# Turning the short row blocks of experts 2 to 7 in pairs, and issuing gathers ahead of the older scatter

## What is computed

```python
x = x + gnn(layernorm(x), adj, W, a1, a2)          # attention over 1354 x 1354, float32
n = layernorm(x)                                    # 1354 x 512
probs = softmax(n @ Wr + br)                        # 8 experts
gate, idx = max(probs), argmax(probs)
pos = rank of the token among those of its expert   # tokens with pos >= 169 are dropped
expert_in[e, pos] = gate * n[token]                 # for the tokens of expert e
h  = relu(expert_in @ W1[e] + b1[e])                # 512 -> 512
eo = h @ W2[e] + b2[e]                              # 512 -> 512
out = x + gate * eo[idx, pos]                       # back to the token's row
```

## Time and profile before

| | us |
|---|---|
| median of 3 timed executions | 265.56 (265.4 to 267.12) |
| the profiled execution, its device time | 263.48 |
| its span in the profile | 261.7 |
| PE busy | 250.5 |
| DVE busy | 180.9 |
| ACT busy | 128.6 |
| POOL busy | 90.1 |

### The profile page before, as it was taken

How to read it: one execution, slowest core, us unless ns; L and a number is a source line. 1 busy time by engine, 2 the same in 40 slices (tenths; PEclk the granted TensorE clock), 3 DMA queues, 4 the chain that set the end, 5 groups by cost and what they waited for, 6 DMA issues and landing times.

```text
span 261.7 us, 4579 instructions
## 1 busy us (share of the span) xinstructions
PE 250.5 (96%) x1649; PEld 210.8 (81%) x1649; DVE 180.9 (69%) x429; ACT 128.6 (49%) x263; POOL 90.1 (34%) x113
## 2 busy tenths in 40 slices
PE   6799989999999999999999999999999999999990
PEld 1489989988888778778778889899977968879780
DVE  3988768996978977785762573847296685856931
ACT  2737786853765475555553121342447155454330
POOL 4334891000341432112120224118253834841502
PEclk9999999999999999999999999999999999999999
DMA  6990000320488888421211213136978679888001
GB/s 189 375 318 32 1 5 0 106 81 27 159 210 284 273 262 248 168 79 40 80 42 41 82 39 96 52 117 176 353 237 294 247 258 290 283 293 285 12 7 44
DMA packets 19210, 40.47 MB, mean 155 GB/s; under 512 B 2810, under 2 KB 3130, under 8 KB 19188
## 3 DMA queue, kind: packets, MB, share of 16 engines
q1 hardware_dynamic: 16196, 34.17, 39.5%
q0 software_dynamic: 2176, 4.80, 6.1%
q10 hardware_dynamic: 816, 1.21, 1.5%
HBM read 32.93 MB, written 8.31 MB: 158 GB/s over the span
## 4 chain that ended last, share of the span: by engine, by line
PE 87%; POOL 3%; DVE 2%; DMA 2%; issue 2%; ACT 2%; POOLq 1%; ACTq 0%
PE bank L1426 30%; PE bank L1690 12%; PE bank L1728 7%; PE bank L1364 6%; PE bank L1412 5%; PE bank L1756 5%; PE bank L1441 3%; PE bank L1660 2%; PE bank L1346 2%; DMA w_raw<-in_L_gnn_W_dram 2%; PE bank L1676 2%; PE bank L1703 2%; PE bank L1453 2%; PE bank L1464 2%; PE bank L1560 1%
## 5 line engine op out<-in xcount | busy, mean ns | idle before, releaser
L1426 PE MATMUL bank<-h_hi,pt_lo 128*128 128x512 f32 (+1 forms) x110 | 45.9, 417 | 0.0
L1426 PE MATMUL bank<-h_lo,pt_hi 128*128 128x512 f32 (+1 forms) x110 | 43.6, 396 | 0.0
L1426 PE MATMUL bank<-h_hi,pt_hi 128*128 128x512 f32 (+1 forms) x110 | 43.4, 394 | 0.0
L411 POOL TENSOR_TENSOR x_all<-x_all,w_raw 128x512 f32<-128x512 f32 x10 | 18.1, 1810 | 65.2 <-ACT w_raw L589 65.2
L1690 PE MATMUL bank<-prob,w 128*128 128x168 f32 x224 | 33.2, 306 | 0.0
L1690 PEld LDWEIGHTS bank<-prob,w 128*128 128x128 f32 x224 | 32.6, 189 | 0.7 <-issue 0.2
L754 ACT ACTIVATE adj_s<-bank,b_cols 128x168 f32<-128x168 f32 x28 | 11.3, 402 | 33.6 <-PE bank L1690 33.6
L1426 PEld LDWEIGHTS bank<-h_hi,pt_hi 128*128 128x128 f32 (+1 forms) x110 | 20.7, 188 | 4.9
L1426 PEld LDWEIGHTS bank<-h_hi,pt_lo 128*128 128x128 f32 (+1 forms) x110 | 20.7, 188 | 3.8
L1426 PEld LDWEIGHTS bank<-h_lo,pt_hi 128*128 128x128 f32 (+1 forms) x110 | 20.8, 189 | 3.6
L611 ACT ACTIVATE wide<-adj_s,off_b 128x1354 f32<-128x1354 f32 (+1 forms) x11 | 15.8, 1432 | 14.1 <-DVE off_b L887 14.1
(11 more groups left out here) (203 smaller groups left out, 558.1 us busy)
## 6 DMA issues: line engine op xcount, KB each, us to landing
w<-in_L_ffn_W_dram SPq DMA_DIRECT2D x16, 1024.0 KB, 6.7
adj_s<-in_adj_dram SPq DMA_DIRECT2D x10, 677.0 KB, 5.3
x_rows<-x_all SPq DMA_DIRECT2D x10, 257.0 KB, 3.2
out_dram<-x_all SPq DMA_DIRECT2D x10, 256.0 KB
x_all<-in_x_dram SPq DMA_DIRECT2D x9, 256.0 KB, 5.6
prob<-in_L_ffn_b_dram SPq DMA_DIRECT2D x5, 256.0 KB, 7.2
w_raw<-in_L_gnn_W_dram ACTq DMA_DIRECT2D x4, 256.0 KB, 5.5
adj_s<-in_L_ffn_b_dram SPq DMA_DIRECT2D x2, 256.0 KB, 7.0
```

The lines of the kernel that those rows point to most:

```text
L411: pool.tensor_tensor(x_all[0:R, t, 0:D], x_all[0:R, t, 0:D], relu_s[0:R, :], ALU.add).then_inc(s_x1, 1)
L1426: ins = pe.matmul(o_ps[par][0:R, :], p[0:K, par, k, 0:R], h[0:K, k, :], start=(k == 0 and n == 0), stop=(k == NT - 1 and n == 2))
```

## The change

The short blocks of experts 2 and 3, 4 and 5, 6 and 7 are put one under the other, in rows 0 to 39 and 64 to 103 of one tile, and turned as one block of PAIR = 104 rows, in the in_turn of the even expert. Expert 1 has its short block turned alone, in a block of the same 104 rows of which only the first 40 are used. The odd experts 3, 5 and 7 have only their wide block turned. To that end:
- PE: in_turn(e) has four transposes of 128 rows to bank 0, and for e = 1, 2, 4, 6 four of 104 rows to bank 1.
- DVE: prepare(e) scales the wide block by itself as soon as it has landed, and for e = 1, 2, 4, 6 then the short block or both short blocks of the pair. Scales are made one column at a time. The new counter is `s_xgt`; `s_xg` is left to expert 0.
- ACT: gx_copy(e) is one instruction of 128x512 for the wide block and, for e = 1, 2, 4, 6, one of 128x(4x40) for each short block. Its wait on `s_hid` is 2e where it was 2e - 2.
- POOL: gathers are issued by block. The short block of expert 3 is gathered with those of expert 2, and so on (two new semaphores, `s_x1n`). In the loop the wait for `s_gt` and the gathers stand ahead of scatter_out(e - 4).
- SP: the wait ahead of the weight loads is for the wide block of expert 1 alone (16 where it was 32).

```diff
@@ buffers and banks
-        xg = w_raw[:, :, 0:D].rearrange("p (i j) n -> p i j n", i=2)
+        xg_w, xg_n = (w_raw[:, 0, 0:D], w_raw[:, 2, 0:D]), (w_raw[:, 1, 0:D], w_raw[:, 3, 0:D])
+        PAIR = P // 2 + CAP - P
-        gx_ps, hid_ps, eo_ps, y_ps = ((banks[0], banks[1]), (banks[2], banks[3]),
-                                      (banks[4], banks[5]), (banks[6], banks[7]))
+        gxw_ps, gxn_ps = banks[0], banks[1]
+        hid_ps, eo_ps, y_ps = (banks[2], banks[3]), (banks[4], banks[5]), (banks[6], banks[7])
+        s_x1n = [sem("s_x1n0"), sem("s_x1n1")]
+        s_xgt = sem("s_xgt")
+        def late(e):
+            return () if e > 1 and e % 2 else (e,) if e == 1 else (e, e + 1)
+        def prepared(e):
+            return e + (e | 1) if e else 0
@@ SP
-            sp.wait_ge(s_x1g[1], 32)
+            sp.wait_ge(s_x1g[1], 16)
@@ POOL
-            def gather_x1(e):
-                for j in range(2):
-                    pool.indirect_dma_start(x1_g[e][0:S[j], j, :], None, x1_d,
-                                            bass.IndirectOffsetOnAxis(ap=src[0:S[j], j, e:e + 1], axis=0)
-                                            ).then_inc(s_x1g[e], 16)
+            def gather_x1(e, j):
+                pool.indirect_dma_start(x1_g[e][0:S[j], j, :], None, x1_d,
+                                        bass.IndirectOffsetOnAxis(ap=src[0:S[j], j, e:e + 1], axis=0)
+                                        ).then_inc(s_x1n[e // 2 % 2] if j and e else s_x1g[e], 16)
-            gather_x1(1)
-            gather_x1(2)
-            pool.wait_ge(s_x1g[1], 32)
+            gather_x1(1, 0)
+            gather_x1(1, 1)
+            gather_x1(2, 0)
+            gather_x1(2, 1)
+            gather_x1(3, 1)
+            pool.wait_ge(s_x1g[1], 16)
+            pool.wait_ge(s_x1n[0], 16)
             pool.wait_ge(s_xg, 2)
-            gather_x1(0)
+            gather_x1(0, 0)
+            gather_x1(0, 1)
             for e in range(3, E + 2):
+                if e < E:
+                    pool.wait_ge(s_gt, e - 1)
+                    gather_x1(e, 0)
+                    for i in late(e):
+                        gather_x1(i, 1)
                 if e >= 4:
                     scatter_out(e - 4)
-                if e < E:
-                    pool.wait_ge(s_gt, e - 1)
-                    gather_x1(e)
@@ ACT
             def gx_copy(e):
+                act.wait_ge(s_gt, e + 1)
+                act.wait_ge(s_hid, 2 * e)
+                ins = act.activation(gx_t[e % 2][:, :, 0:P], gxw_ps[:, :].rearrange("p (c n) -> p c n", c=KC), ACT.Copy)
+                for i, n in enumerate(late(e)):
+                    v = gxn_ps[:, 0:KC * PAIR].rearrange("p (c n) -> p c n", c=KC)
+                    ins = act.activation(gx_t[n % 2][:, :, P:CAP], v[:, :, P // 2 * i:P // 2 * i + S[1]], ACT.Copy)
                 ins.then_inc(s_gxt, 1)
@@ DVE, prepare(e)
-                dve.wait_ge(s_x1g[e], 32)
+                dve.wait_ge(s_gt, max(e - 1, 1))
+                dve.wait_ge(s_x1g[e], 16)
+                dve.tensor_tensor(scale_s[:, par, 0:1], x1_g[e][:, 0, D + 1:D + 2], gate_s[:, 0, e:e + 1], ALU.mult
                                   ).then_inc(s_scale, 1)
+                dve.wait_ge(s_scale, 2 + prepared(e - 1))
+                dve.tensor_scalar(xg_w[par], x1_g[e][:, 0, 0:D], x1_g[e][:, 0, D:D + 1], scale_s[:, par, 0:1],
+                                  ALU.subtract, ALU.mult).then_inc(s_xgt, 1)
+                if late(e):
+                    dve.wait_ge(s_x1n[e // 2 % 2], 16 * (e // 2 + 1))
+                    for n in late(e):
+                        dve.tensor_tensor(scale_s[0:S[1], n % 2, 1:2], x1_g[n][0:S[1], 1, D + 1:D + 2],
+                                          gate_s[0:S[1], 1, n:n + 1], ALU.mult).then_inc(s_scale, 1)
+                    dve.wait_ge(s_scale, 1 + prepared(e))
+                    for i, n in enumerate(late(e)):
+                        dve.tensor_scalar(xg_n[e // 2 % 2][P // 2 * i:P // 2 * i + S[1], :], x1_g[n][0:S[1], 1, 0:D],
+                                          x1_g[n][0:S[1], 1, D:D + 1], scale_s[0:S[1], n % 2, 1:2],
+                                          ALU.subtract, ALU.mult).then_inc(s_xgt, 1)
@@ PE, in_turn(e)
-                pe.wait_ge(s_xg, e * 2 + 2)
+                pe.wait_ge(s_xgt, prepared(e))
                 pe.wait_ge(s_gxt, e)
-                for j in range(2):
+                for c in range(KC):
+                    ins = pe.transpose(gxw_ps[:, c * P:(c + 1) * P], xg_w[e % 2][:, c * P:(c + 1) * P], ident[:, :])
+                if late(e):
                     for c in range(KC):
-                        o = (c % 2) * CAP
-                        ins = pe.transpose(gx_ps[c // 2][:, o + j * P:o + j * P + S[j]],
-                                           xg[0:S[j], e % 2, j, c * P:(c + 1) * P], ident[0:S[j], 0:S[j]])
+                        ins = pe.transpose(gxn_ps[:, c * PAIR:(c + 1) * PAIR],
+                                           xg_n[e // 2 % 2][0:PAIR, c * P:(c + 1) * P], ident[0:PAIR, 0:PAIR])
                 ins.then_inc(s_gt, 1)
```

More of the change, by code:

```diff
@@ L698, in _, with gx_copy_first @@
             exp_below(2)
-            def gx_copy(e):
[L701 to L704, removed]
-                for j in range(2):
[L706 to L712, removed]
+            def gx_copy_first():
+                for j in range(2):
+                    act.wait_ge((s_gt0, s_gt)[j], 1)
+                    act.activation(gx_t[0][:, 2 * j:2 * j + 2, :],
+                                   gx0_ps[j][:, 0:2 * CAP].rearrange("p (c n) -> p c n", c=2), ACT.Copy
+                                   ).then_inc((s_gx0, s_gxt)[j], 1)
+            def gx_copy(e):
+                act.wait_ge(s_gt, e + 1)
[4 more added lines that the diff above has]
+                    ins = act.activation(gx_t[n % 2][:, :, P:CAP], v[:, :, P // 2 * i:P // 2 * i + S[1]], ACT.Copy)
                 ins.then_inc(s_gxt, 1)
@@ L756, in hid_relu @@
                     ins.then_inc(s_hidv, 1)
-            gx_copy(0)
+            gx_copy_first()
             act.wait_ge(s_bc, 1)
@@ L1201, in out_bias @@
                     v = x1_g[e][0:S[j], j, 0:D]
-                    dve.wait_ge(s_xg, e * 2 + j + 1)
+                    dve.wait_ge(s_xgt, prepared(e))
                     dve.scalar_tensor_tensor(v, b2_b[i][0:S[j], :], gate_s[0:S[j], j, e:e + 1], v, ALU.mult, ALU.add
```

## The result

| | before | after |
|---|---|---|
| median of 20 timed executions | 265.63 us | 262.99 us |
| profiled execution, device time | 263.48 us | 262.5 us |
| its span | 261.7 us | 260.8 us |

The account below looks back on a forecast made before the run. PE was taken to bound the kernel; 1.65 us from the odd turns plus 0.68 from the other four gave 2.33 us off, nothing elsewhere: 265.56 - 2.33 = 263.2 us, ratio 0.991, range 262.3 to 265.2.

Parts of the forecast that it names:

- PE's bound and the odd turns: PE sets the pace; leaving the short block out of turns 3, 5 and 7 saves 0.55 us each, 1.65 us.
- The even turns: PE, turns 2, 4 and 6: a 104-row block for one of 40 takes 1.06 us for 1.23, saving 0.17 each.
- Expert 1: PE, turn of expert 1, followed by out_turn_first: the same saving of 0.17 us assumed for its 104-row block.
- The landing at expert 2: prepare(2) needs a third block: short gather lands at 186.2 to 186.9 us, stall 0; bound 1.4 us.
- C: prepare(2) late in part, landing between 187.0 and 189.2: at 188.3 a stall of 1.4 us, 264.6 us; chance 0.18.
- D: Landing for in_turn(2) so late, past 189.25, that the kernel is slower than before; chance 0.04.
- SP's earlier start: SP's weight loads of expert 2 wait for one block and start about 0.85 us earlier; 0 us for PE.
- The moved gathers: POOL issues gathers ahead of the scatter, expert 4's 5.4 us earlier; 0 us from the earlier issue.
- What would show it: Signs for right or wrong, among the latter a PE wait at wide_part for hid_low in an even period, costed at nothing.
- DVE and ACT elsewhere: Even prepares some 0.9 us longer, covered by hid_low(3)'s 1.42 us wait; ACT at most 0.7 more, with 4.41 idle.
- B: PE's even turns: the 104-row block has the breaks too, 0.97 us gained, 264.6 us; chance 0.10.
- E: PE's pause before the second layer stays, only the short slots go: 0.3 us gained, 265.3 us; chance 0.03.

Follow-up runs that it names:

- the run with the late gather: Changed kernel with the gather of expert 3's short block issued after the second gather of expert 0, 2.5 us later; ratio 1.0144.
- the kernel with the scatter first: Changed kernel with POOL's loop in the old order, the older scatter ahead of the wait and gathers; ratio 0.9996, again 0.9932.
- the run with both waits: Changed kernel with SP's weight loads of expert 2 again waiting for both blocks of expert 1; ratio 0.9882, of 4 executions.
- the kernels with 64, 72 and 104 rows: Kernel before with each expert's short block turned by itself over 64, 72 or 104 rows, no gather moved; ratios 1.0018, 0.9942 and 0.9932.
- the one without short blocks: Kernel before with the short block's four transposes left out of all seven turns, no gather moved; ratio 0.9917.

## Why the prediction was right, point by point

- **PE's bound and the odd turns.** 3 x 0.55 was forecast; counted in the chains from one turn to the next, the three periods fell by 0.56, 0.56 and 0.55 us, 1.67 in all. Right.
- **The even turns.** 1.05 us for the forecast 1.06. The periods that begin with turns 2, 4 and 6 fell by 0.18, 0.20 and 0.19 us for 0.17, 0.57 in all for 0.51. Right, and the interpolation between 74 and 128 rows held.
- **Expert 1.** This term was mis-sized. I took the same 0.17; from the start of the stretch to the end of the first layer of expert 1 it was 188.44 - 177.03 = 11.41 us before by the chain and 189.69 - 178.30 = 11.39 after, so it is worth 0.02. There the first layer follows the turn after only eight transposes, and it waits for ACT, whose copies of 512 and 160 columns end 0.15 us before it (184.72, the first layer from 184.87). I had costed ACT by the 4.41 us behind a copy in mid-stage, which isn't the cover at expert 1.
- **The sum.** 1.67 + 0.57 + 0.02 = 2.26 us for 2.33. That it came so close is in part luck: the 0.15 us lost at expert 1 was half made up by 0.06 and 0.02 more at the other turns. The forecast of the profiled execution, 261.15 us, was 1.35 too low, because that execution lost 1.27 us ahead of the stretch. The timed median, 262.99 for 263.2, was met.
- **The landing at expert 2.** I took a stall of 0, which it was, with 0.78 us of cover by the chain and 0.48 by the weight loads; the forecast's landing times gave 0 to 0.7. The price of a late landing was mis-sized: rivals C and D put it at its own length, and the run with the late gather shows 1.8 us of slow clock on top of a wait of 3.6. For a wait as short as C's 1.4 no run shows such a sequel by itself: after PE's wait of 1.2 us in the kernel with the scatter first the clock stayed at 1.00.
- **SP's earlier start.** 0.85 us earlier was forecast, at no cost to PE. It was 0.6 us earlier (1.78 us into the stretch for 2.37) and cost PE nothing, but by the run with both waits it made expert 2's wide block land some 3.1 us later.
- **The moved gathers.** "0 us for the earlier issue" was right for the edit alone. What I did not ask is what it costs if that cover is gone: without it, 1.4 us of the 2.3 in the profiles. That what DVE waits for lies beside PE work held for before, and not for the faster kernel in the old order; the sum held because the changed kernel has the new one. I had looked for the danger at the turns, while the first thing to be late was hid_low behind prepare(4), which "What would show it" names and costs at nothing.
- **DVE and ACT elsewhere.** In period 3 the longer prepare(4) used up the 1.42 us that hid_low(3) had waited; it was done at 209.26, and PE wanted it at 210.3. Right.
- **Rivals B and E** are out by the kernels with 64, 72 and 104 rows and the one without short blocks.
- **The chance.** Faster by over 1% was put at 0.29; the ratio is 0.992, just inside the bound.

## What to carry to other kernels

When PE sets the pace, price a small matmul by the starts around it and look for idle weight loads at its edges: a block of 64 rows or fewer between full ones cost more here than one of 72 or 104. A faster bottleneck can use up the slack of what feeds it, so an edit that brings nothing by itself, like issuing the gathers earlier, can be what keeps the gain of another; ask first of the work that is queued behind the one that is fed. A stall of the matrix engine can cost more than its length, when the granted clock falls behind it.

## What the runs showed of the hardware

- The break at the edges of a short block is there at 64 rows and gone at 72: 1.39 us from the first load to the second layer's third with 64, 1.11 with 72.
- After 4 us with PE nearly idle the granted clock was 0.72 and 0.71 in the next 6 us; after waits of 0.4 and 1.8 us it was 0.52 over 3 us; after waits of 1.5 and 2.0 us it stayed at 1.00. What decides between them is open.
- Gathers on the chain landed 7.0 to 7.1 us after issue while weight loads ran, and 9.3 and 9.4 us in the kernels without short blocks and with 72 rows alone, where the same gather took 6.2 us in before and 6.6 with 104 rows.
- Whether a gather is issued ahead of a weight load or into it matters: with one wait of SP changed, expert 2's wide block was there 5.4 us into the stretch, when POOL was done with its gather 0.2 us ahead of the load's issue, and 8.5 us into it, when the load was issued while POOL was at the gather.
